# Token shares of the second feed-forward: turned in steps 6 to 12 of the block attention, from copies kept among the constants

## The chip, the cores and the metric

The kernel runs on one core of a Trainium2 chip. The metric is the device time of one execution in microseconds (us), the median over several runs. The engines are TensorE (PE in the profile; its weight loads are PEld), VectorE (DVE), ScalarE (ACT), GpSimd (POOL) and SyncE (SP), which only issues transfers here. Each runs its own list of instructions in order and waits on semaphores.

## The reference

Two transformer layers over x of 4 x 256 tokens by 256. Each layer adds an attention and a mixture of experts to x. The change lies in the second layer:

```
xn = layernorm(x)
# attention: 16 heads of 16, keys in blocks of 32 tokens, each query sees its 4 best blocks
mask   = selected blocks & causal
p      = softmax(where(mask, q @ k.T * d**-0.5, NEG));  o = p @ v
o      = o * rsqrt(mean(o*o)) * o_norm_w;  attn = o @ Wo.T
# feed-forward: 8 experts of rank 32, two for each token
rw, sel = top_k(softmax(x @ Wg.T), 2);  rw = rw / rw.sum(-1)
for k in range(2):
    x1, x3 = base1 + lora1[sel[:, k]], base3 + lora3[sel[:, k]]
    x2  = silu(x1) * x3
    out += (x2 @ W2.T + lora2(x2)) * rw[:, k]
```

The two numbers rw of a token are its shares. The kernel multiplies x2 by them while the tokens lie along the free axis, so it needs each share repeated over all 128 partitions.

## The kernel before, in words

All is written out by hand: each engine has a function with its instructions in order, and semaphores order the work between them. No planner moves anything.

At the end of the second layer's preparation VectorE chooses the two experts and forms `share` (line 1748). It then writes the block scores (lines 1753 to 1756, the last of them steps the semaphore `blk_step` to 3) and ranks the blocks: 7 comparisons of the first batch's heads (`compare`, line 691), 14 additions and subtractions (`count`, lines 700 and 702), and four comparisons of the other heads. GpSimd copies `share` into `share_rep`, each share repeated 128 times along the free axis: two copies of 1024 elements per partition (line 905). It goes on with its own rankings once VectorE has done all seven comparisons of the other heads, then with masks, with the splitting of the expert weights `b13` into a high and a low part (lines 924 and 927), and with further splits for the feed-forward.

The block attention runs over steps j = 0 to 34. A step has two heads, n = 2j and 2j + 1, and four heads (two steps) make a quad Q. On TensorE a step is: the scores of its heads (`scores1`, lines 2206 and 2212); in odd steps from 3 the products with the values of quad (j - 3) // 2 (`values1`, line 2233); the turning of the probabilities of the step before (`probs1_turn`, line 2222, six transposes); in even steps from 4 the turning of a quad's output (`quad_turn`, line 2241). ScalarE in a step takes the exponents of one head (`exponents`, line 1198, two instructions), copies the turned probabilities of the even head (line 1204), takes the exponents of the other head, and in some steps scales the next queries (`own_queries`, line 1167), forms the next block bias (`own_bias`, line 1178) and copies a quad's output (`quad_out`, line 1214). VectorE adds the bias to the scores and takes their minimum (`masked_minimum`, line 1774), copies the odd head's turned probabilities (line 1783) and divides the quad's heads (`heads_out`, lines 1789 and 1792).

Into the first steps the kernel puts the shares. TensorE turns `share_rep` by four transposes for a quarter of it (`shares(n)`, line 2341) into a PSUM bank, and ScalarE copies the bank to `shareT` (`share_out(n)`, line 1208), which the feed-forward reads. `share_rep` lies in the same place as the later slots of `probs1T`, the turned probabilities, so it has to be read before they are written. Quarter 0 uses bank 2 and quarters 1 to 3 bank 7, which are also the two banks of the values and the quad outputs. In step 5 TensorE waits until all four quarters have left their banks. Scores use banks 3, 4, 0 and 1, turned probabilities banks 5 and 6.

Behind step 31 TensorE goes straight on to the feed-forward's hidden layer (`hidden1`), which wants GpSimd's splits.

Of the kernel before, what the change touches and what calls it, by code (L numbers as in the profile page):

```python
# [15 lines left out]
ACT = mybir.ActivationFunctionType  # L16
AX = mybir.AxisListType

P = 128
B, S, D = 4, 256, 256  # L20
TOK = B * S
NT = TOK // P
# [48 lines left out]
HG = H1 // 2  # L71
QUADS = 2 * GROUPS
VW = D1 + 1
SCORE_BANK, SHARE_BANK = (3, 4, 0, 1), (2, 7, 7, 7)

F1, E1, R1 = 896, 8, 32
ER = E1 * R1
# [1 line left out]
CH = 512  # L79
# [56 lines left out]
B3_AT = -(-CF["q_cos"][0] // ALIGN) * ALIGN  # L136
# [160 lines left out]
def program(nc, t, y):  # L297

    ctx = ExitStack()
    with ctx:  # L300
# [31 lines left out]
        with ExitStack() as overlay:  # L332
            end = 0
            kept, phase = -(-(CF_N + BC_N + NT * D) // ALIGN) * ALIGN, start[1] + 8 * TOK
# [23 lines left out]
        sb = ctx.enter_context(nc.sbuf_tensor("sb", [P, SB_COLS], F32))  # L358
        rd = ctx.enter_context(nc.sbuf_tensor("rounded", [P, ROUNDED], F32))
        cb = ctx.enter_context(nc.sbuf_tensor("cb", [P, CB_N], BF16))  # L360
        bank = [ctx.enter_context(nc.psum_tensor(f"bank{i}", [P, 512], F32)) for i in range(8)]
# [7 lines left out]
        region2 = whole.take(REGIONS[2])  # L369
# [17 lines left out]
        def tableb(name):  # L387
# [3 lines left out]
        ident, identb = table("ident"), tableb("ident")  # L391
# [110 lines left out]
        phase = r2.at  # L502
# [5 lines left out]
        r2 = Strip(region2, phase + 2 * NT * D, NT * D)  # L508
        expert_of = [r2.take_b(NT, ER) for _ in range(2)]
        one_of = [bias_g[:, k].rearrange("p q n -> p (q n)")[:, 0:NT * E1].rearrange("p (t e) -> p t e", e=E1) for k in range(2)]  # L510
        share_rep = Strip(region2, phase + 3 * NT * D, 2 * NT * P).take(2 * NT, P)
        r2 = Strip(region2, phase, region2.shape[1] - phase)
        v_last = r2.take(H1, VW)
        v_one = [v_most[:, i] for i in range(NT - 1)] + [v_last]
# [21 lines left out]
        shareT = r4.take(2, TOK)  # L536
# [13 lines left out]
                           for w in (w13, w13_lo[:, :].rearrange("p (k n) -> p k n", k=KD)))  # L550
# [56 lines left out]
        kmean_set, kmean_done, blk_mm, blk_step = (sem(n) for n in ("kmean_set", "kmean_done", "blk_mm", "blk_step"))  # L607
# [4 lines left out]
        fill_mm, fill_out, step_mask, low_rank = (sem(n) for n in ("fill_mm", "fill_out", "step_mask", "low_rank"))  # L612
        bl_q, bl_bias, bl_s, bl_min, bl_exp, bl_inv, bl_t, bl_even, bl_odd, bl_v, bl_oT, bl_turn, bl_o = (
            sem(n) for n in ("bl_q", "bl_bias", "bl_s", "bl_min", "bl_exp", "bl_inv", "bl_t", "bl_even", "bl_odd", "bl_v",
                             "bl_oT", "bl_turn", "bl_o"))
# [17 lines left out]
        def fills():  # L633

            out = [("low", j, h, c) for j in range(2) for h in range(2) for c in range(TOK // CH)]
            return out + [("mask", k, h, c) for k in range(2) for h in range(2) for c in range(TOK // CH)]
# [164 lines left out]
        def _(pool):  # L801
# [8 lines left out]
            for u in range(2 * NF):  # L810
                n = P if u // 2 < NF - 1 else FH
# [69 lines left out]
            for i in range(NT):  # L881
# [3 lines left out]
                if i >= HALF:  # L885
                    n, k = (i - HALF) // KD, (i - HALF) % KD
# [14 lines left out]
            for q in range(QT):  # L901
                pool.tensor_copy(ranks_b[:, q], along(table("later", QT, NB)[:, q], (1, B), (2, H1))).then_inc(kmean_set, 1)
            pool.wait_ge(r1_step, 10 + 2 * NT)
            for k in range(2):
                pool.tensor_copy(share_rep[:, k * NT:(k + 1) * NT, :], along(share[:, :, k], (2, P))).then_inc(r1_share, NT)

# [12 lines left out]
                pool.tensor_tensor(am_step[j], am_step[j], step_maskT, ALU.mult).then_inc(low_rank, 1)  # L919

            pool.wait_ge(ab_in, 48)
            for j in range(2):
                for h in range(2):
                    pool.tensor_copy(r(b13_hi[j][h]), b13[:, h, j * F1:(j + 1) * F1]).then_inc(b13_split, 1)
                for h in range(2):
                    pool.wait_ge(b13_split, 4 * j + h + 1)
                    pool.tensor_tensor(r(b13_lo[j][h]), b13[:, h, j * F1:(j + 1) * F1], b13_hi[j][h], ALU.subtract)\
                        .then_inc(b13_split, 1)
# [31 lines left out]
        def _(act):  # L960
# [63 lines left out]
            for u in range(2, 2 * NF):  # L1024
# [3 lines left out]
                if 0 <= u - 3 < NT:  # L1028
                    i = u - 3
# [171 lines left out]
            def even_probsT(n):  # L1201
                act.wait_ge(bl_t, n + 1)
                at_least(act, bl_v, n // 4 - 1)
                act.activation(probs1T[:, n % 8, :], bank[5][:, 0:3 * P], ACT.Copy).then_inc(bl_even, 1)

            def share_out(n):
                act.wait_ge(fill_mm, len(fills()) + n + 1)
                act.activation(shareT[:, n // 2, n % 2 * CH:(n % 2 + 1) * CH], bank[SHARE_BANK[n]][:, :], ACT.Copy)\
                    .then_inc(fill_out, 1)

            def quad_out(Q):
# [18 lines left out]
            for j in range(2 * QUADS + 3):  # L1230
                if j < 2 * QUADS:
                    exponents(2 * j)
                if 0 < j <= 2 * QUADS:
                    even_probsT(2 * j - 2)
                if j == 2 * QUADS:
                    act.wait_ge(bl_s, GROUPS * HG)
                    act.wait_ge(w3_in, 32)
                    high_part("w13", 1)
                    high_part("w13", 2)
                    activated(0, 0)  # L1240
                if j < 2 * QUADS:
                    exponents(2 * j + 1)
                if 0 < j < 5:
                    share_out(j - 1)
                if j % 4 == 2 and j // 4 + 1 < GROUPS:
                    own_queries(j // 4 + 1)
                if j % 4 == 3 and j // 4 + 1 < GROUPS:
                    own_bias(j // 4 + 1)
                if j % 2 and j > 2:
                    quad_out((j - 3) // 2)  # L1250
# [621 lines left out]
        def _(pe):  # L1872
# [14 lines left out]
            for i in range(NT):  # L1887
# [5 lines left out]
                for k in range(KD):  # L1893
                    mm = pe.matmul(bank[4 + i % 2][:, 0:LATX], xnT[:, k, i * P:(i + 1) * P], w_lat[:, k, 0:LATX],  # L1894
                                   start=(k == 0), stop=(k == KD - 1))
# [31 lines left out]
            for u in range(2 * NF):  # L1927
                shared_up(u)
                if u == 2 * NF - 2:
# [5 lines left out]
                    for i in range(NT - 1):  # L1935
                        mm = pe.matmul(bank[6][:, (i + 1) * E0:NT * E0].rearrange("p (t e) -> p t e", e=E0),
                                       tableb("ones"), along(maskb[:, i, :], (1, NT - 1 - i)),
                                       start=False, stop=(i == NT - 2), skip_group_check=True)
# [132 lines left out]
            for i in range(NT):  # L2071
# [9 lines left out]
                for f in range(NF):  # L2081
                    mm = pe.matmul(bank[DOWN_BANK[i]][:, 0:D], hT[:, f, i * P:(i + 1) * P], sw_down[:, f, :],  # L2082
                                   start=(f == 0), stop=(f == NF - 1))
# [13 lines left out]
                if i == NT - 2:  # L2097
                    for j in range(NT * TOPK0):
                        if j % HOT == 0:
                            pe.wait_ge(rt_mask, j // HOT + 2)  # L2100
                        mm = pe.matmul(bank[7][:, 0:2 * E0].rearrange("p (h e) -> p h e", h=2), hot[:, j, :], ids[:, :, j, :],
                                       start=(j == 0), stop=(j == NT * TOPK0 - 1))
# [112 lines left out]
            def probs1_turn(n):  # L2215
                pe.wait_ge(bl_exp, 2 * n + 2)
                if n % 2:
                    at_least(pe, bl_odd, (n - 1) // 2)
                else:
                    at_least(pe, bl_even, n // 2)  # L2220
                for j in range(3):
                    mm = pe.transpose(bank[5 + n % 2][:, j * P:(j + 1) * P], probs1[:, n % 4, j * P:(j + 1) * P], ident)  # L2222
                mm.then_inc(bl_t, 1)

            def values1(Q):
                G, b, k, par, i = place_of(4 * Q)
                pe.wait_ge(bl_even, 2 * Q + 2)
                pe.wait_ge(bl_odd, 2 * Q + 2)
                at_least(pe, bl_o, Q - 1)
                for t_ in range(QT):  # L2230
                    for i in range(4):
                        dst = bank[2 + 5 * (Q % 2)][32 * i:32 * i + VW, t_ * P:S]
                        mm = pe.matmul(dst, v_one[QT * b + t_][:, HG * k + 2 * i + par, :],
                                       probs1T[:, (4 * Q + i) % 8, 2 * t_ * P:(2 + t_) * P],
                                       start=(t_ == 0), stop=(t_ == 1))
                mm.then_inc(bl_v, 1)
# [99 lines left out]

            def shares(n):
                pe.wait_ge(r1_share, 4 * n + 4)
                pe.wait_ge(fill_out, len(fills()) + (n if n > 1 else 0))
                for i in range(4):  # L2340
                    mm = pe.transpose(bank[SHARE_BANK[n]][:, i * P:(i + 1) * P], share_rep[:, 4 * n + i, :], ident)
                mm.then_inc(fill_mm, 1)

            pe.wait_ge(fill_out, len(fills()) - 3)
# [2 lines left out]
            for j in range(2 * QUADS + 3):  # L2347
                if j < 2 * QUADS:
                    scores1(j)
                if j == 1:  # L2350
                    shares(0)
                    shares(1)
                if j in (3, 4):
                    shares(j - 1)
                if j == 5:
                    pe.wait_ge(fill_out, len(fills()) + 4)
                if j % 2 and j > 2:
                    values1((j - 3) // 2)
                if 0 < j <= 2 * QUADS:
                    probs1_turn(2 * j - 2)  # L2360
                    probs1_turn(2 * j - 1)
                if j == 2 * QUADS:
                    hidden1(0)
                if j == 2 * QUADS + 1:
                    hidden1(1)
                if j % 2 == 0 and j > 3:
                    quad_turn((j - 4) // 2)
# [37 lines left out]
```

## Time and profile before

| what | value |
|---|---|
| median of 3 runs | 700.69 us (700.65 to 703.05) |
| the profiled execution | 701.29 us, of which the span from first to last instruction is 699.1 us |
| busy in the span | PE 96%, DVE 70%, ACT 61%, POOL 43% |
| granted TensorE clock | 1.00 |
| the block attention, from TensorE's first scores to its last probabilities | 408.0 to 493.6 us |

In a row of the timeline the first number is the start in us from the span's start, the second the length in us, then engine, line, operation, tiles and shapes, and the count of instructions that the row merges; in brackets stands how long the engine was idle before it and what released it. A record begins when the instruction is taken up, and the next one often begins before the end of the one before: what an instruction costs its engine is read from start to start. In a row of the windows stand the stretch and its length, then busy time and count of PE, PEld, DVE, ACT and POOL, then the granted clock, the DMA share and GB/s.

### The profile page before, as it was taken

Reading aid. Unit: us, or ns where it says so; the run is one execution under the profiler, and the core shown is the slowest. Engines: PE = TensorE matmul, PEld = TensorE weight load, DVE = VectorE, ACT = ScalarE, POOL = GpSimd, SP = SyncE. Lnnn points to the kernel's source line nnn. Section 1 sums busy time; section 2 is a strip of 40 time slices with the busy share of each in tenths; the row PEclk is TensorE's granted clock in tenths of the full one; section 3 lists DMA queues with packets and bytes.
Section 4 is the critical chain, followed back from the end, with each engine's and each line's share of the span. In section 5 each row is a group of like instructions: output and inputs, shape, how many; then the busy total and the mean of one; then the engine's idle time right before and its main releaser. Section 6 shows DMA issues by size and latency. Waiting matters only on the chain.

```text
span 699.1 us, 13847 instructions
## 1 busy us (share of the span) xinstructions
PE 671.0 (96%) x4756; PEld 581.7 (83%) x4756; DVE 489.0 (70%) x1418; ACT 424.3 (61%) x1099; POOL 297.8 (43%) x301
## 2 busy tenths in 40 slices
PE   6999999999999999999999989999989999999997
PEld 3777888888889898887787855666889999999997
DVE  6798877877877787777786886777465555644544
ACT  3766168788797878888663788888654213222221
POOL 0584154546464555542164318998334410400000
PEclk9999999999999999999999999999999999999999
DMA  8902044453535444351910000200300000000000
GB/s 329 346 1 98 1 130 121 165 166 112 168 116 165 129 152 126 101 159 59 365 79 1 1 1 2 107 1 3 121 1 1 1 1 16 2 16 1 1 16 16
DMA packets 26725, 59.43 MB, mean 85 GB/s; under 512 B 3146, under 2 KB 12748, under 8 KB 26272
## 3 DMA queue, kind: packets, MB, share of 16 engines
q1 hardware_dynamic: 23584, 50.35, 21.5%
q0 software_dynamic: 3072, 8.20, 3.6%
q8 instruction: 39, 0.64, 0.4%
q14 instruction: 30, 0.25, 0.1%
HBM read 48.24 MB, written 10.49 MB: 84 GB/s over the span
## 4 chain that ended last, share of the span: by engine, by line
PE 76%; DVE 14%; ACT 6%; issue 3%; POOL 1%; DMA 0%; DVEq 0%; ACTq 0%
PE bank L2253 11%; PE bank L2020 7%; PE bank L1954 6%; PE bank L2302 5%; PE bank L2011 5%; PE bank L2276 5%; PE bank L2040 4%; PE bank L1961 3%; PE bank L2031 3%; PE bank L2082 3%; PE bank L2316 2%; PE bank L2222 2%; PE bank L2206 2%; PE bank L1894 2%; PE bank L2161 2%
## 5 line engine op out<-in xcount | busy, mean ns | idle before, releaser
L1062 ACT ACTIVATE sb<-bank,sb 128x256 f32<-128x256 f32 x128 | 59.6, 471 | 40.6 <-DVE sb L1558 33.4
L1558 DVE TENSOR_REDUCE sb<-bank 128x2 f32<-128x512 f32 x64 | 43.7, 683 | 47.5 <-PE bank L2020 47.1
L1264 ACT ACTIVATE h_parts<-sb 128x256 fp32r<-128x256 f32 x56 | 23.4, 418 | 71.3 <-DVE sb L1809 43.4
L2020 PE MATMUL bank<-sb 128*128 128x256 f32 x256 | 66.2, 381 | 0.0
L1800 DVE TENSOR_TENSOR sb<-sb,bank 128x256 f32<-128x256 f32 x56 | 23.5, 419 | 58.1 <-ACT sb L1227 58.1
L2253 PE MATMUL bank<-rounded,b_hi 128*128 128x256 f32 x224 | 63.1, 282 | 0.0
L2253 PE MATMUL bank<-rounded,b_lo 128*128 128x256 f32 x224 | 62.9, 281 | 0.0
L2253 PE MATMUL bank<-am_lo,b_hi 128*128 128x256 f32 x224 | 62.9, 281 | 0.0
L1227 ACT ACTIVATE sb<-bank 128x256 f32<-128x256 f32 x56 | 21.5, 383 | 62.4 <-PE bank L2253 62.4
L834 POOL DMA_INDIRECT expert_out<-sb x32 | 33.0, 1032 | 61.0 <-DVE sb L1500 44.6
L1069 ACT ACTIVATE sb<-sb 128x256 f32<-128x256 f32 x128 | 57.7, 503 | 0.1
L1198 ACT ACTIVATE sb<-sb 128x128 f32<-128x128 f32 (+1 forms) x128 | 50.6, 445 | 10.1 <-DVE sb L1774 9.4
L1954 PEld LDWEIGHTS bank<-sb 128*128 128x128 f32 (+1 forms) x384 | 46.5, 186 | 5.8 <-DVE sb L1494 3.2
L828 POOL DMA_INDIRECT sb<-rows_x,sb x32 | 32.8, 1025 | 42.4 <-PE bank L1954 16.4
L1954 PE MATMUL bank<-sb 128*128 128x128 f32 (+1 forms) x384 | 48.8, 277 | 1.7 <-DVE sb L1494 1.0
L2020 PEld LDWEIGHTS bank<-sb 128*128 128x128 f32 x256 | 45.2, 190 | 4.8
L1774 DVE CUSTOM_DVE_ANT_1 sb<-bank,sb 128x128 f32<-128x128 f32 (+1 forms) x128 | 38.0, 353 | 12.8 <-ACT sb L1178 8.5
L1569 DVE TENSOR_TENSOR pt_parts<-bank,pt_parts 128x512 fp32r<-128x512 f32 x64 | 43.7, 683 | 4.5 <-ACT pt_parts L1082 3.6
L2040 PE MATMUL bank<-pt_parts,xt_parts 128*128 128x256 f32 x256 | 46.0, 302 | 0.0
L1811 DVE TENSOR_TENSOR h_parts<-sb,h_parts 128x256 fp32r<-128x256 f32 x56 | 25.9, 462 | 27.4 <-ACT h_parts L1264 27.4
L2011 PE MATMUL bank<-rounded 128*128 128x512 f32 x160 | 42.7, 399 | 0.3 <-ACT sb L1091 0.3
L2253 PEld LDWEIGHTS bank<-rounded,b_lo 128*128 128x128 f32 x224 | 42.2, 188 | 0.0
(321 smaller groups left out, 1969.9 us busy)
## 6 DMA issues: line engine op xcount, KB each, us to landing
sb<-in_w_gate_up SPq DMA_DIRECT2D x32, 368.0 KB
sb<-in_w_down SPq DMA_DIRECT2D x32, 256.0 KB
sb<-in_w_pair SPq DMA_DIRECT2D x8, 704.0 KB
expert_out<-sb SPq DMA_DIRECT2D x1, 4096.0 KB, 23.7
sb<-expert_out SPq DMA_DIRECT2D x8, 512.0 KB, 6.3
sb<-in_w SPq DMA_DIRECT2D x1, 1792.0 KB, 13.8
sb<-in_b SPq DMA_DIRECT2D x1, 1792.0 KB, 8.1
sb<-in_sw_up SPq DMA_DIRECT2D x1, 1536.0 KB, 9.4
```

The source lines that it names most:

```text
L1062: act.activation(probs[:, u % 4, q, :], bank[3 + u % 2][:, q * S:(q + 1) * S], ACT.Exp, scale=-1.0, bias=row_min[:, u % 4, q:q + 1], accum ...
L1069: ins = act.activation(probs[:, slot, q, :], probs[:, slot, q, :], ACT.Copy, scale=row_inv[:, slot, q:q + 1])
L1198: act.activation(probs1[:, n % 4, a:b], masked[:, n % 4, a:b], ACT.Exp, scale=-1.0, bias=row_min[:, n % 4, q:q + 1]).then_inc(bl_exp, 1)
L1558: dve.tensor_reduce(row_min[:, u % 4, :], bank[3 + u % 2][:, :].rearrange("p (q n) -> p q n", q=QT), AX.X, ALU.min).then_inc(at_min, 1)
L1569: dve.tensor_tensor(r(probs_lo[:, u % 2]), bank[5 + u % 2][:, :].rearrange("p (a b) -> p a b", a=QT), probs_hi[:, u % 2], ALU.subtract).th ...
L1774: dve.tensor_tensor_reduce(masked[:, n % 4, a:b].rearrange("p (n c) -> p n c", c=CHUNK), bank[SCORE_BANK[n % 4]][:, a:b].rearrange("p (n c ...
L1954: mm = pe.matmul(bank[1][0:n, to:to + P], w_gu[s][:, k, a:a + n], xeT[s][:, k, :], start=(k == 0), stop=(k == KD - 1))
L2011: mm = pe.matmul(where[:, :], r(w[i][:, cols]), r(q[:, half]), start=(n == 0), stop=(n == len(terms) - 1))
L2020: mm = pe.matmul(bank[3 + u % 2][:, q * S:(q + 1) * S], qb[i][:, h, b * S + q * P:b * S + (q + 1) * P], keys[:, h, b * S:(b + 1) * S], sta ...
L2040: mm = pe.matmul(bank[2 + 5 * h][:, 0:S], r(v_parts[:, QT * b + k, :]), r(part[:, u % 2, k, :]), start=(n == 0), stop=(n == len(terms) - 1))
L2253: mm = pe.matmul(dst, lhs, rhs, start=False, stop=(n == len(terms) - 1), skip_group_check=True)
L2276: pe.matmul(dst, r(w[:, 2 * k + j, :]), r(x[:, k, :]), start=(i + j == 0), stop=False, skip_group_check=True)
```

## The change

`share_rep` moves from the place under `probs1T` to the columns of the constants from `B3_AT` on: rotation tables, block masks and layer-norm rows that are done with by then. Later the same columns take the high parts of `b13` (second half) and one tile of another weight. GpSimd's two copies therefore wait until VectorE has read the block masks (`blk_step` 3), and GpSimd waits, ahead of splitting `b13`, until all four quarters have been turned. The quarters are turned in steps 6, 8, 10 and 12 instead of 1, 1, 3 and 4, alternately in banks 2 and 7, right behind the scores; each waits until the quad that had the bank is done (`bl_o`). ScalarE copies a quarter in the same step, between its copy of the turned probabilities and the second exponents. In steps 7, 9, 11 and 13 TensorE first turns the probabilities, then waits for the quarter's copy and forms the values; in the other odd steps the order stays.

```diff
-SCORE_BANK, SHARE_BANK = (3, 4, 0, 1), (2, 7, 7, 7)
+SCORE_BANK = (3, 4, 0, 1)
+SHARE_AT = {6: 0, 8: 1, 10: 2, 12: 3}
...
-        share_rep = Strip(region2, phase + 3 * NT * D, 2 * NT * P).take(2 * NT, P)
+        share_rep = Strip(sb, B3_AT, 2 * NT * P).take(2 * NT, P)
...
             pool.wait_ge(r1_step, 10 + 2 * NT)
+            pool.wait_ge(blk_step, 3)
             for k in range(2):
                 pool.tensor_copy(share_rep[:, k * NT:(k + 1) * NT, :], along(share[:, :, k], (2, P))).then_inc(r1_share, NT)
...
             pool.wait_ge(ab_in, 48)
+            pool.wait_ge(fill_mm, len(fills()) + 4)
...
             def share_out(n):
                 act.wait_ge(fill_mm, len(fills()) + n + 1)
-                act.activation(shareT[:, n // 2, n % 2 * CH:(n % 2 + 1) * CH], bank[SHARE_BANK[n]][:, :], ACT.Copy)\
+                act.activation(shareT[:, n // 2, n % 2 * CH:(n % 2 + 1) * CH], bank[2 + 5 * (n % 2)][:, :], ACT.Copy)\
                     .then_inc(fill_out, 1)
...
                     even_probsT(2 * j - 2)
+                if j in SHARE_AT:
+                    share_out(SHARE_AT[j])
...
                     exponents(2 * j + 1)
-                if 0 < j < 5:
-                    share_out(j - 1)
...
             def shares(n):
                 pe.wait_ge(r1_share, 4 * n + 4)
-                pe.wait_ge(fill_out, len(fills()) + (n if n > 1 else 0))
+                pe.wait_ge(bl_o, n + 1)
                 for i in range(4):
-                    mm = pe.transpose(bank[SHARE_BANK[n]][:, i * P:(i + 1) * P], share_rep[:, 4 * n + i, :], ident)
+                    mm = pe.transpose(bank[2 + 5 * (n % 2)][:, i * P:(i + 1) * P], share_rep[:, 4 * n + i, :], ident)
                 mm.then_inc(fill_mm, 1)
...
                 if j == 1:
-                    shares(0)
-                    shares(1)
-                if j in (3, 4):
-                    shares(j - 1)
-                if j == 5:
-                    pe.wait_ge(fill_out, len(fills()) + 4)
-                if j % 2 and j > 2:
+                    pe.wait_ge(fill_out, len(fills()))
+                if j in SHARE_AT:
+                    shares(SHARE_AT[j])
+                behind_shares = j - 1 in SHARE_AT
+                if j % 2 and j > 2 and not behind_shares:
                     values1((j - 3) // 2)
                 if 0 < j <= 2 * QUADS:
                     probs1_turn(2 * j - 2)
                     probs1_turn(2 * j - 1)
+                if behind_shares:
+                    pe.wait_ge(fill_out, len(fills()) + SHARE_AT[j - 1] + 1)
+                    values1((j - 3) // 2)
```

## Rows read from the trace of the kernel before

**Rows 1.** Windows: one period of four steps, 6 to 9.
```profile
426.12:436.40 10.28, 10.17 (x103) 6.44 (x102) 7.51 (x40) 8.97 (x26) 8.64 (x22) 1.00 0.00 0
```
**Rows 2.** Timeline of PE, steps 1 to 6 and the start of step 10.
```profile
410.25 1.04 PE L2341 MATMUL bank<-sb 128*128 128x128 f32 x8
411.95 1.24 PE L2222 MATMUL bank<-sb 128*128 128x128 f32 x6 [0.67 <-ACT sb L1198]
413.12 0.92 PE L2206 MATMUL bank<-sb 32*128 32x128 f32 x8
...
417.47 0.63 PE L2341 MATMUL bank<-sb 128*128 128x128 f32 x4 [1.27 <-ACT sb L1208]
...
421.19 0.63 PE L2341 MATMUL bank<-sb 128*128 128x128 f32 x4 [0.34 <-ACT sb L1208]
421.66 0.82 PE L2222 MATMUL bank<-sb 128*128 128x128 f32 x6
422.31 0.38 PE L2241 MATMUL bank<-sb 128*128 128x128 f32 x2
...
424.54 0.84 PE L2233 MATMUL bank<-sb 128*17 128x256 f32 x16 [0.67 <-ACT sb L1208]
425.32 0.87 PE L2222 MATMUL bank<-sb 128*128 128x128 f32 x6
426.12 0.92 PE L2206 MATMUL bank<-sb 32*128 32x128 f32 x8
...
436.30 0.92 PE L2206 MATMUL bank<-sb 32*128 32x128 f32 x8
```
**Rows 3.** Timeline of ACT, steps 0 to 2.
```profile
411.10 2.18 ACT L1198 ACTIVATE sb<-sb 128x128 f32<-128x128 f32 x6 [1.42 <-DVE sb L1774]
...
416.75 0.58 ACT L1208 ACTIVATE sb<-bank 128x512 f32<-128x512 f32 x1
417.22 0.90 ACT L1167 ACTIVATE sb<-sb 128x256 f32<-128x256 f32 x2
```
**Rows 4.** Timeline of ACT, steps 6 to 8.
```profile
427.98 0.80 ACT L1198 ACTIVATE sb<-sb 128x128 f32<-128x128 f32 x2 [0.63 <-DVE sb L1774]
428.68 0.47 ACT L1204 ACTIVATE sb<-bank 128x384 f32<-128x384 f32 x1
429.05 0.79 ACT L1198 ACTIVATE sb<-sb 128x128 f32<-128x128 f32 x2
429.75 0.90 ACT L1167 ACTIVATE sb<-sb 128x256 f32<-128x256 f32 x2
430.55 0.79 ACT L1198 ACTIVATE sb<-sb 128x128 f32<-128x128 f32 x2
...
432.30 0.39 ACT L1178 ACTIVATE sb<-sb 128x128 f32<-128x128 f32 x1
...
433.49 0.80 ACT L1198 ACTIVATE sb<-sb 128x128 f32<-128x128 f32 x2 [0.54 <-DVE sb L1774]
```
**Rows 5.** Timeline of DVE and POOL around the copies, before the first step.
```profile
399.72 1.05 POOL L905 COPY sb<-sb 128x1024 f32<-128x1024 f32 x1
...
400.01 1.82 DVE L1756 TENSOR_TENSOR sb<-sb 128x1024 f32<-128x1024 f32 x1
...
407.94 2.56 DVE L691 TENSOR_TENSOR sb<-sb 128x672 bf16<-128x672 f32 x4
```
**Rows 6.** Timeline, elsewhere: DVE with two SBUF inputs, first or behind POOL.
```profile
357.47 2.05 POOL L889 TENSOR_TENSOR w_qkvg_lo<-sb,w_qkvg_hi 128x776 fp32r<-128x776 f32 x1
...
357.86 1.94 DVE L1669 SCALAR_TENSOR_TENSOR sb<-sb 128x256 f32<-128x256 f32 x1
...
531.54 1.22 DVE L1857 TENSOR_TENSOR sb<-sb 128x1024 f32<-128x1024 f32 x1
```
**Rows 7.** Timeline of POOL: before its rankings, first split of b13, before the feed-forward.
```profile
416.14 0.60 POOL L700 TENSOR_TENSOR sb<-sb 128x224 f32<-128x224 f32 x1 [15.37 <-DVE sb L691]
...
457.64 1.81 POOL L924 CAST b_hi<-sb 128x896 fp32r<-128x896 f32 x2
...
494.23 2.52 POOL L956 TENSOR_TENSOR w_lo<-sb,w_hi_rest 128x512 fp32r<-128x512 f32 x2 [6.67 <-ACT w_hi_rest L1219]
```

## The prediction, made before the changed kernel was run

> **What bounds the kernel now.** I read the page first, for the shares of the engines, and then the chain of work that ended last. TensorE has most of that chain over the whole span, so the question is only what the change does to TensorE's time between its first scores and the hidden layer behind step 31. The windows of that stage come next. In a period of four steps TensorE is busy 10.17 of 10.28 us and ScalarE 8.97 [rows 1]: from step 6 on TensorE is the bound, and ScalarE is not far behind. The period is 10.18 us, from the scores of step 6 at 426.12 to those of step 10 at 436.30, while steps 2 to 5 took 13.00 us, from 413.12 to 426.12 [rows 2]. The timeline says why: in these steps TensorE is idle three times for the copy of a quarter, 1.27, 0.34 and 0.67 us [rows 2]. The reader is to see two regimes: early steps with holes, later ones without.
>
> The timeline of VectorE shows a third thing. It has no gap ahead of the first minimum: its last four comparisons run from 407.94 for 2.56 us [rows 5], the first minimum follows at once, at about 410.4, and ScalarE was idle 1.42 us for it before the first exponents at 411.10 [rows 3], for which TensorE in turn was idle 0.67 us [rows 2]. So whatever delays VectorE ahead of step 0 delays the whole stage.
>
> **What is removed from the early steps.** Quarters 0 and 1 in step 1 (eight transposes, 410.25 to 411.29) lie in a hole: TensorE had to wait until 411.95 for exponents anyway [rows 2]. Removing them gives nothing. Quarter 2 in step 3 costs its wait of 1.27 us and about 0.5 of transposes, quarter 3 in step 4 costs 0.34 and 0.47 (421.19 to 421.66), and step 5 waits 0.67 [rows 2]: some 3.3 us on TensorE, the most that can be won. What comes up in its place are the waits that every later period has: steps 2 and 3 hold the same scaled queries and bias on ScalarE as steps 6 and 7. I therefore take the period of 10.18 as what steps 2 to 5 will need, and the gain as 13.00 - 10.18 = 2.8 us. It was 0 if another wait filled these holes. Against that: ScalarE's copies of the quarters (0.47 us each, from 416.75 to 417.22 [rows 3]) leave its list there as well, and the probabilities that the values of step 3 want were copied before the hole of 1.27 us had ended.
>
> **What is added to steps 6 to 13.** On TensorE each quarter is four transposes, 0.47 us by the distance to the next row [rows 2], and TensorE has 0.11 us of idle time in a period. The four cost at least 4 x 0.47 = 1.9 us. The changed order makes it a little more, because the second transposes of a step now wait for exponents that ScalarE takes behind a quarter's copy, with no values in front of them to cover that. Worked out on ScalarE, which sets the pace there:
>
> - Steps 6 and 7. From the exponents at 427.98 to those at 433.49 are 5.51 us of exponents (0.70), copy (0.37), exponents (0.70), queries (0.80) and so on; the last piece, from the bias at 432.30 by way of VectorE's minimum, is 1.19 us [rows 4]. Up to the bias ScalarE has no gap. The quarter's copy adds 0.47 and nothing absorbs it: +0.5.
> - Steps 8 and 9. From the exponents at 433.49 to the scores of step 10 at 436.30 were 2.81 us. After the change the path is: exponents 0.70, copy 0.37, quarter 0.47, exponents 0.70 [rows 3, 4], then on TensorE half of the six transposes, 0.33 of 0.65 (421.66 to 422.31), and the values, 0.78 (424.54 to 425.32) [rows 2], with some 0.05 from engine to engine: 3.4 us. That is +0.6.
>
> Together 1.1 us for four steps, 2.2 us for steps 6 to 13. The other bound is that every quarter is paid with a wait like that of step 5 on top of its transposes, 4 x (0.47 + 0.67) = 4.6 us. I take 2.2, since it follows the new order of instructions. The waits on `bl_o` cost nothing: quad 0 is divided in step 4 and quarter 0 asks in step 6, and so on two steps apart. From step 14 on the order is the old one.
>
> One page of the Trainium skill would give another price. "TensorE: Matmul & The Clock Gate", in its part on PE-mode transpose, gives about 275 ns for one transpose in a kernel. The records here have the same length, but four of them start within 0.47 us of each other and the next work. Taken one after another, 16 x 0.275 = 4.4 us would be an estimate from that page, and the sum would be 2.2 us higher than mine; the distance between rows decides.
>
> **The copies on GpSimd.** They are two instructions of 1.05 us. Before, the second ran from 399.72 to 400.77, and VectorE's L1756, taken up at 400.01, needed 1.82 us, where the same shape in L1857 needed 1.22 [rows 5, 6]. It ended 1.06 us behind the copy: it stood still until the copy was over. The same is seen at L1669: taken up at 357.86 beside GpSimd's L889, which ended at 359.52, it ended at 359.80 [rows 6]. In both cases VectorE has two inputs in SBUF and GpSimd reads SBUF too. After the change the copies start behind L1756, so this one gets back 0.6 us. They then run beside the seven comparisons and the additions of the ranking, which all have two inputs in SBUF. The comparison that is under way holds GpSimd for a moment, then a copy holds the next comparison, and at its end the turn changes again; L889 took its turn in this way between two instructions of VectorE. So both copies are paid: 2 x 1.05, less about 0.1 for the overlap, = 2.0 us. With the 0.6 regained VectorE reaches the first minimum 1.4 us later, at 411.8, and the stage starts 1.4 us later. The bounds are -0.6 (VectorE keeps its turn until it is through) and +1.5. I take 1.4.
>
> The Trainium skill, "SBUF — State Buffer", in "Who interferes with whom", says the same of a VectorE instruction with two SBUF inputs beside a GpSimd instruction that reads SBUF: one is blocked for the whole of the other. No row has a comparison (L691) beside a GpSimd instruction, and the page puts it with the others. By it the sum would be 2.1 for 2.0 us; a reading in which bf16 outputs escape would take away 2.0.
>
> **What costs nothing.** GpSimd's own list: the copies move some 2.5 us later into a wait of 15.37 us [rows 7]. That wait ends with VectorE's last comparison in step 2, so the rankings and all behind them start 1.4 us later too; ahead of the feed-forward GpSimd then waited another 6.67 us [rows 7]. Its new wait for the fourth quarter stands before the splitting of `b13` at 457.64 [rows 7], when step 12 (half a period behind step 10, about 441) is long past; were it ever late, the splits would hold the hidden layer. SyncE has no new wait; its weights for the feed-forward are released by the last scores and move with the stage.
>
> **The sum.** -2.8 + 2.2 + 1.4 = +0.8 us in the span: 699.1 becomes 699.9, and the profiled execution 702.1. That execution was 0.6 us above the median of the runs; on the median 700.69 I forecast 701.4 us, +0.1%.
>
> **Rivals.**
>
> 1. The comparisons aren't held by the copies. For it: GpSimd has no priority that the rows show, and each comparison is short. Against: L1756 and L1669. Then -2.8 + 2.2 - 0.6 = -1.2: 699.4 us.
> 2. The quarters cost more than the order of instructions says, 4.6 us instead of 2.2, because ScalarE (8.97 of 10.28 us busy) becomes the bound in steps 6 to 13. Against: 0.47 us in two steps still fits into its idle time by count. Then +3.2: 703.9 us.
> 3. The early steps don't get shorter: VectorE's and ScalarE's start-up sets steps 2 to 5, and the holes stay under other names. Then 0 + 2.2 + 1.4 = +3.6: 704.3 us, slower by 0.5%. It decides from the point where less than 0.1 us of the 2.8 is won. Against: all three holes name the copy of a quarter.
> 4. The moved work is free and the copies too: -2.8 - 0.6, 697.3 us. TensorE's 0.11 us of idle time speaks against it.
>
> **How the numbers follow.** The forecast with small shifts of its terms 0.62, rival 1 0.16, rival 2 0.12, rival 3 0.06, rival 4 0.04. The range takes in the forecast, rival 1, the lower half of rival 2, and a run-to-run change of a few tenths: 699.1 to 703.1. By 0.5% (3.5 us), about what a measurement of this kernel can tell from no change, only rival 3 and a worse rival 2 are slower, and only a rival 4 with more is faster: faster 0.02, same 0.92, slower 0.06.
>
> **What the profile after should show.** No idle time of TensorE for L1208 in steps 2 to 5, and about 10.2 us from the scores of step 2 to those of step 6. About 11.3 us each for steps 6 to 9 and 10 to 13, with TensorE idle 0.8 to 0.9 us ahead of the turned probabilities in steps 9 and 13, released by L1198, and 10.2 us again from step 14. L1756 at 1.2 us; two comparisons or additions behind it with 1 us more than before; the first minimum at about 411.8. Wrong would be: comparisons of unchanged length, periods of over 12 us with quarters, or a first period still near 13 us.

## The result: 0.65% slower, and where the time went

The changed kernel takes 705.24 us (median of 9 runs, 704.36 to 709.56), the kernel before 700.69 us in 9 runs beside it. The ratio is 1.0065, 95% interval 1.0053 to 1.0077: 4.6 us slower, where 701.4 us (699.1 to 703.1) was forecast. The profiled execution took 704.72 us with a span of 702.8 us, 3.7 us more than before. Eight of the nine executions took 704.4 to 705.5 us with a mean granted clock of 0.992, the ninth 709.56 us with 0.983.

All of it lies in the block attention. The windows of the kernel after, in the columns explained above: from the first scores to the first turned probabilities, then the rest of steps 1 to 3 and the start of 4, steps 4 and 5, and the periods 6 to 9, 10 to 13 and 14 to 17.

```profile
407.48:412.60 5.12, 2.43 (x20) 1.28 (x21) 4.96 (x19) 2.61 (x7) 0.00 (x0) 0.90 0.01 2
412.60:422.20 9.60, 9.58 (x55) 5.95 (x55) 5.02 (x27) 6.05 (x17) 3.72 (x8) 0.52 0.01 3
422.20:427.02 4.82, 4.82 (x52) 3.18 (x51) 3.74 (x20) 4.13 (x13) 4.04 (x11) 1.00 0.00 0
427.02:438.52 11.50, 10.75 (x110) 7.25 (x109) 8.19 (x41) 10.45 (x31) 9.70 (x24) 1.00 0.01 2
438.52:450.02 11.50, 10.74 (x112) 7.25 (x108) 7.64 (x40) 9.83 (x29) 11.34 (x5) 1.00 0.44 162
450.02:460.20 10.18, 10.07 (x104) 6.33 (x100) 6.95 (x39) 8.36 (x25) 10.18 (x4) 1.00 0.01 2
```

The third number from the end of a row is the granted clock. In the second row it is 0.52 while TensorE is busy all the time: for some 9 us it ran at 1.2 instead of 2.4 GHz. The 0.90 of the first row is about 1.0 us more of it, at the end of the hole. That is what no step of the prediction had. The timeline of TensorE shows what it had done before, beside [rows 2]:

```profile
407.48 0.92 PE L2209 MATMUL bank<-sb 32*128 32x128 f32 x8
...
412.62 1.51 PE L2225 MATMUL bank<-sb 128*128 128x128 f32 x6 [2.71 <-ACT sb L1201]
414.06 1.65 PE L2209 MATMUL bank<-sb 32*128 32x128 f32 x8
...
419.58 1.48 PE L2236 MATMUL bank<-sb 128*17 128x256 f32 x16
...
427.02 0.92 PE L2209 MATMUL bank<-sb 32*128 32x128 f32 x8
...
431.27 0.55 PE L2225 MATMUL bank<-sb 128*128 128x128 f32 x3 [0.19 <-ACT sb L1201]
...
437.27 0.55 PE L2225 MATMUL bank<-sb 128*128 128x128 f32 x3 [0.56 <-ACT sb L1201]
...
438.52 0.92 PE L2209 MATMUL bank<-sb 32*128 32x128 f32 x8
```

The hole ahead of the first turned probabilities is 2.71 us long instead of 0.67: the eight transposes of quarters 0 and 1 are gone from it, and VectorE is later. The scores of step 2 then take 1.65 us instead of 0.92, and none of the holes for a quarter's copy is left in steps 2 to 5. Still these steps take 12.96 us (414.06 to 427.02) where they took 13.00. The timeline of VectorE and GpSimd around the copies, beside [rows 5]:

```profile
399.51 1.22 DVE L1759 TENSOR_TENSOR sb<-sb 128x1024 f32<-128x1024 f32 x1
400.77 3.22 DVE L692 TENSOR_TENSOR sb<-sb 128x224 bf16<-128x224 f32 x7
...
411.00 0.28 DVE L1777 CUSTOM_DVE_ANT_1 sb<-bank,sb 128x128 f32<-128x128 f32 x1
```
```profile
400.89 2.29 POOL L907 COPY sb<-sb 128x1024 f32<-128x1024 f32 x2 [11.46 <-DVE sb L1759]
```

The last addition to the block scores is back at 1.22 us (1.82 before), and the seven comparisons beside the copies take 3.22 us.

From row to row the 4.0 us that the stage grew from its first scores to those of step 14 divide so (the stage of before began 0.5 us later in its span, which is why the span grew less):

| stretch, from scores to scores | before | after |
|---|---|---|
| step 0 to 2 | 5.14 | 6.58 |
| step 2 to 6 | 13.00 | 12.96 |
| step 6 to 10 | 10.18 | 11.50 |
| step 10 to 14 | 10.18 | 11.50 |
| step 14 to 18 | 10.18 | 10.18 |

### The profile page after: what moved, and what is told of

It is laid out like the page before. It is cut to its first block, busy times and chain, and to the rows that moved or that the text cites. A ratio compares the mean times of both kernels' runs of the same rounds, so it can differ in the third digit from the quotient of the medians.

```text
span 702.8 us, 13853 instructions
## 1 busy us (share of the span) xinstructions
PE 673.7 (96%) x4756; PEld 584.1 (83%) x4756; DVE 490.2 (70%) x1418; ACT 424.0 (60%) x1099; POOL 297.9 (42%) x301
## 4 chain that ended last, share of the span: by engine, by line
PE 73%; DVE 16%; ACT 6%; issue 4%; POOL 1%; DMA 0%; DVEq 0%; ACTq 0%
PE bank L2256 11%; PE bank L2023 7%; PE bank L1957 6%; PE bank L2305 5%; PE bank L2014 5%; PE bank L2279 5%; PE bank L2043 3%; PE bank L1964 3%; PE bank L2034 3%; PE bank L2085 3%; PE bank L2225 2%; PE bank L2319 2%; PE bank L2209 2%; PE bank L2164 2%; PE bank L1897 2%
## 5 line engine op out<-in xcount | busy, mean ns | idle before, releaser
L1201 ACT ACTIVATE sb<-sb 128x128 f32<-128x128 f32 (+1 forms) x128 | 50.4, 446 | 14.6 <-DVE sb L1777 14.4
```

Of the source, the lines that this page charges most:

```text
L1201: act.activation(probs1[:, n % 4, a:b], masked[:, n % 4, a:b], ACT.Exp, scale=-1.0, bias=row_min[:, n % 4, q:q + 1]).then_inc(bl_exp, 1)
```

## The experiments

Theory A: the hole on TensorE makes the clock fall, and the low clock takes the gain of steps 2 to 5. Rival B: VectorE and ScalarE set steps 2 to 5 whatever the clock, or the clock falls for something else. Ratios are to the kernel before, with 95% intervals; the table below has the stretches of each profile.

**Eight transposes put back.** The kernel after with

```diff
                 if j == 1:
                     pe.wait_ge(fill_out, len(fills()))
+                    for i in range(8):
+                        pe.transpose(bank[2 + 5 * (i // 4)][:, i % 4 * P:(i % 4 + 1) * P], ident, ident)
```

> The kernel after, with eight transposes of the identity in step 1, where the two quarters stood before; their results are never read. Theory A (the clock): the hole ahead of the first turned probabilities was 2.71 us long and the granted clock fell behind it, to a mean of 0.52 for 9.6 us. Eight transposes make the hole about 1.7 us, the clock stays at 1.00, steps 2 to 5 take 10.2 us instead of 12.96 and the first turning another 0.3 less: 705.2 - 3.1 = 702.1 us. Rival B (start-up): steps 2 to 5 take 13 us because VectorE and ScalarE set them, whatever the clock: 705.2 us.

Measured: 703.71 us (12 runs), 1.0023 [1.0011, 1.0034]. The hole was 1.76 us and the clock fell nevertheless, but later:

```profile
412.00:416.00 4.00, 3.13 (x21) 2.38 (x22) 3.36 (x21) 3.37 (x10) 0.00 (x0) 0.86 0.00 0
416.00:420.00 4.00, 4.00 (x30) 1.70 (x28) 2.45 (x13) 3.21 (x9) 2.77 (x5) 0.50 0.00 0
```

So A's forecast failed in the profile: with a hole of 1.76 us the clock still fell. But the profiled execution is one of eight, at 703.3 to 704.3 us and a mean clock of 0.994 or 0.995; the other four took 701.9 to 702.5 us, about the 702.1 of theory A, at 0.999. With this hole the clock falls in most executions and not in all. B isn't excluded by the profile, since steps 2 to 5 took 12.49 us.

**Copies later on GpSimd.** The kernel after with

```diff
             pool.wait_ge(blk_step, 3)
+            pool.wait_ge(bl_min, 1)
```

> The kernel after, with GpSimd's two copies held back until the first minimum of step 0 is done, when no VectorE instruction with two SBUF inputs is under way. Theory A: the seven comparisons take 1.5 us again instead of 3.2, L1759 keeps its 1.22, the first minimum comes 2.3 us behind the first scores instead of 3.5, the hole on TensorE is about 1.4 us and the clock stays at 1.00. The sum against before is -2.8 (steps 2 to 5) - 0.5 (first minimum) + 2.6 (steps 6 to 13, two periods of 11.50 instead of 10.18) = -0.7: 700.0 us. Rival B: steps 2 to 5 stay at 13 us, 702.8 us. If a hole of 1.4 us without any transposes in it is enough for the clock to fall: about 703.

Measured: 703.28 us (12 runs), 1.0029 [1.0014, 1.0044]. The part about VectorE came true; its timeline:

```profile
399.97 1.23 DVE L1760 TENSOR_TENSOR sb<-sb 128x1024 f32<-128x1024 f32 x1
401.23 1.56 DVE L692 TENSOR_TENSOR sb<-sb 128x224 bf16<-128x224 f32 x7
...
410.37 0.28 DVE L1778 CUSTOM_DVE_ANT_1 sb<-bank,sb 128x128 f32<-128x128 f32 x1
410.58 0.42 DVE L1778 CUSTOM_DVE_ANT_1 sb<-bank,sb 128x256 f32<-128x256 f32 x1
```
```profile
410.27 2.03 POOL L908 COPY sb<-sb 128x1024 f32<-128x1024 f32 x2 [20.37 <-DVE sb L1778]
```

The comparisons take 1.56 instead of 3.22 us with nothing but the time of the copies changed, and the minima (L1778), which run beside the copies now, have the 0.28 of the kernel after. The hole shrank to 1.08 us, but the clock fell again, and for longer (the mean was 0.50 from 412.3 to 425). So the 700.0 us were missed and the last sentence of the expectation, about 703 us, came true. The profiled execution took 706.43 us, one of four at 705.6 to 706.4 us (mean clock 0.988 or 0.989); the other eight took 702.3 to 703.5 us (0.992 or 0.993), so the 15.51 us in the table below is the worse kind.

**The place alone.** The kernel before with `share_rep` in the constants and GpSimd's two waits:

```diff
-        share_rep = Strip(region2, phase + 3 * NT * D, 2 * NT * P).take(2 * NT, P)
+        share_rep = Strip(sb, B3_AT, 2 * NT * P).take(2 * NT, P)
...
+            pool.wait_ge(blk_step, 3)
...
+            pool.wait_ge(fill_mm, len(fills()) + 4)
```

> The kernel before with one part of the change: the repeated shares among the constants, with the two waits on GpSimd that go with it. The quarters stay in steps 1, 1, 3 and 4. Theory A: the copies hold VectorE as in the kernel after, the first minimum is 1.1 us later, the hole on TensorE grows from 0.67 to 1.7 us, the clock stays at 1.00: 700.7 + 1.1 = 701.8 us. If a hole of 1.7 us is enough for the clock: some 3 us more, 704.8. If the copies' delay is absorbed: 700.7.

Measured: 703.50 us (12 runs), 1.0025 [1.0015, 1.0034]. The hole became 1.76 us:

```profile
412.85 1.24 PE L2224 MATMUL bank<-sb 128*128 128x128 f32 x6 [1.76 <-ACT sb L1200]
414.02 0.92 PE L2208 MATMUL bank<-sb 32*128 32x128 f32 x8
...
416.40 1.65 PE L2208 MATMUL bank<-sb 32*128 32x128 f32 x8
```

Steps 0 and 1 took 6.24 us instead of 5.14: the copies' price is 1.1 us. And the clock fell here too, with every quarter where it had been. This part alone makes the kernel slower, by 0.25%; the 704.8 us that the expectation gave for a fallen clock were more than was measured.

**The quarter's copy behind the second exponents.** The kernel with late copies and

```diff
                     even_probsT(2 * j - 2)
-                if j in SHARE_AT:
-                    share_out(SHARE_AT[j])
...
                     exponents(2 * j + 1)
+                if j in SHARE_AT:
+                    share_out(SHARE_AT[j])
```

> As the kernel with late copies, and ScalarE copies a quarter behind the second exponents of its step instead of ahead of them. TensorE's second transposes in steps 7, 9, 11 and 13 then don't wait for the quarter; the values behind them do. By the order of instructions that saves 0.2 us in steps 7 and 11 and 0.3 to 0.5 us in steps 9 and 13, about 1 us: 699.0 us where the late copies alone give 700.0. Rival: the quarter's 0.48 us on ScalarE is on the path wherever it stands: no difference between the two.

Measured: 703.08 us (12 runs, 697.69 to 704.33), 1.0001 [0.9981, 1.0020]. The periods with quarters took 11.03 us instead of 11.50, 0.95 us in all, as expected: the place of the copy in ScalarE's list has its price. The total tells little, since ten executions took 701.2 to 704.3 us (mean clock 0.990 to 0.993) and two 697.7 and 697.9 (1.000). In the profiled one, of the long kind, the clock was down behind a hole of 1.05 us:

```profile
409.90:411.10 1.20, 0.15 (x3) 0.04 (x1) 1.20 (x9) 0.95 (x3) 1.18 (x2) 1.00 0.00 0
411.10:421.90 10.80, 10.72 (x60) 6.76 (x62) 5.66 (x28) 7.27 (x21) 5.66 (x11) 0.53 0.01 2
```

**The hole filled.** Three experiments asked whether the clock was all of it. First the kernel after with 20 transposes in the place of 8:

```diff
                 if j == 1:
                     pe.wait_ge(fill_out, len(fills()))
+                    for i in range(20):
+                        pe.transpose(bank[2 + 5 * (i // 4 % 2)][:, i % 4 * P:(i % 4 + 1) * P], ident, ident)
```

> The kernel after, with 20 transposes of the identity in step 1 in place of 8, some 2.5 us of work that nobody reads; it fills the hole of 2.71 us almost wholly. With 8 of them a hole of 1.76 us was left, and the clock fell all the same from 415 on. Theory A (TensorE's idle time between its first scores and the first turned probabilities makes the clock fall, and the clock takes the gain of steps 2 to 5): clock 1.00 throughout the stage, steps 2 to 5 take 10.2 us, median about 701.5 us. Rival B (the clock falls for the work ahead of the first scores, or for the kind of work, transposes among it): it falls again, 704 us or more.

Measured: 701.82 us (11 runs, 701.59 to 702.50), 1.0011 [1.0002, 1.0020]. The timeline and the windows:

```profile
409.79 2.35 PE L2356 MATMUL bank<-sb 128*128 128x128 f32 x20
412.59 1.24 PE L2225 MATMUL bank<-sb 128*128 128x128 f32 x6 [0.45 <-ACT sb L1201]
413.76 0.92 PE L2209 MATMUL bank<-sb 32*128 32x128 f32 x8
```
```profile
407.50:412.60 5.10, 4.62 (x41) 3.50 (x41) 4.93 (x20) 2.58 (x7) 0.00 (x0) 1.00 0.02 5
412.60:423.90 11.30, 10.64 (x104) 6.79 (x104) 8.72 (x47) 9.98 (x29) 6.02 (x15) 1.00 0.00 1
```

The clock stays at 1.00 in the stage, and steps 2 to 5 take 10.18 us. Work that nobody reads makes the kernel 0.54% faster by the ratios, 3.8 us. Rival B falls in each of its forms: nothing on VectorE or ScalarE was changed, nor the work ahead of the first scores, and the added work is transposes.

Then the reverse on the kernel before: two of the eight transposes of quarters 0 and 1 are left in step 1.

```diff
-                for i in range(4):
+                for i in range(4 if n > 1 else 1):
```

> The kernel before, in which quarters 0 and 1 are turned by one transpose each instead of four (six of the eight transposes of step 1 are left out, so half of the tokens' first shares are not formed). Nothing else moves: VectorE and ScalarE have the same times, and the hole ahead of the first turned probabilities grows from 0.67 to about 1.4 us. Theory A: the clock falls, steps 2 to 5 take 14 to 15.5 us instead of 13.0, and the median is 2 to 3 us above before. Rival B (these transposes lay in a hole and are worth nothing, as the prediction had it): the same time as before.

(Of the first shares one in four is formed, not half.) Measured: 703.29 us (6 runs, 702.15 to 705.13), 1.0035 [1.0022, 1.0048]. The windows of the hole, of what follows, of the low clock and of the rest up to step 6:

```profile
409.70:411.00 1.30, 0.01 (x1) 0.01 (x1) 1.30 (x11) 0.87 (x3) 0.00 (x0) 1.00 0.00 0
411.00:417.00 6.00, 4.59 (x36) 2.99 (x36) 4.97 (x27) 5.85 (x16) 1.66 (x3) 1.00 0.01 3
417.00:420.70 3.70, 3.70 (x30) 2.44 (x30) 0.56 (x1) 2.17 (x7) 3.15 (x8) 0.54 0.01 2
420.70:426.10 5.40, 4.81 (x52) 3.13 (x48) 3.29 (x19) 4.26 (x12) 4.54 (x12) 1.00 0.00 0
```

Taking work away made the kernel 2.5 us slower, as theory A said. The profile is of the fastest of the six executions: its steps 2 to 5 took 0.96 us more than before, and the clock fell once more at the start of the feed-forward (last section), so that the time behind the scores of step 14 grew by another 0.9 us. Steps 0 and 1 still took 5.13 us, so the six transposes had indeed lain in a hole, and were not free to remove all the same. The clock did not fall behind the first hole but behind the second, the 1.27 us in step 3 that the kernel before has too [rows 2] and gets over in its profile. Not in each of its executions, it seems: of the 75 of the kernel before that ran beside the experiments, 19 had a mean clock of 0.992 to 0.995 and took 701.9 to 703.3 us. No profile shows where the clock fell in them.

Last, four more transposes in step 1 of the kernel before:

```diff
                     shares(1)
+                    for i in range(4):
+                        pe.transpose(bank[6][:, i * P:(i + 1) * P], ident, ident)
```

> The kernel before with four more transposes of the identity in step 1, 0.5 us for its hole of 0.67 us. The clock didn't fall there in the profile. Theory A: nothing changes in the median, 0 to -0.5 us; a filler that isn't needed costs nothing. Rival: four transposes delay the chain of step 1, +0.5 us.

Measured: 701.19 us (12 runs), 1.0003 [0.9994, 1.0012], the stretches as before. A filler inside a wait costs nothing, and brings nothing where the clock stands. Nor did these four keep the clock up everywhere: five of the twelve executions had a mean clock of 0.993 or 0.995 and took 701.9 to 703.3 us.

**Versions that beat both.** The kernel with late copies and the later quarter's copy, plus the eight transposes of the first experiment:

> The kernel with late copies and the quarter's copy behind the second exponents, plus eight transposes of the identity in step 1, about 1 us, for the hole of 1.05 us. Without them ten of twelve executions took 701.2 to 704.3 us and two took 697.7 and 697.9. Theory A: the clock stays in all of them, steps 2 to 5 take 10.2 us instead of 13.7, and the median is about 698 us, some 0.4% under before: a version that beats both. Rival B: about 703 us as before.

Measured: 699.27 us (11 runs, 697.41 to 699.87), 0.9974 [0.9965, 0.9983]. That is 1.3 us over the forecast: only two executions, 697.4 and 697.7 us, had a mean clock of 1.000; nine had 0.997 or 0.998 and took 698.7 to 699.9. In the profile, one of the nine, the clock stays at 1.00 in this stage and falls at the start of the feed-forward (last section). The hole is filled:

```profile
409.27 1.04 PE L2357 MATMUL bank<-sb 128*128 128x128 f32 x8
410.37 1.24 PE L2226 MATMUL bank<-sb 128*128 128x128 f32 x6
411.54 0.92 PE L2210 MATMUL bank<-sb 32*128 32x128 f32 x8
```

Beside the next one and the unchanged kernel after, on one chip:

> The version with late copies, the quarter's copy behind the second exponents and eight filler transposes, beside the last one on one chip: 0.997 times before, 699.3 us.

Measured: 699.51 us (5 runs), 0.9974 [0.9962, 0.9986]. And with real work as the filler (beside the lines shown, only the addresses of the two places and the waits on `bl_o` differ):

```diff
-SHARE_AT = {6: 0, 8: 1, 10: 2, 12: 3}
+SHARE_AT = {6: 2, 8: 3}
...
-        share_rep = Strip(sb, B3_AT, 2 * NT * P).take(2 * NT, P)
+        share_rep = [Strip(region2, phase + 3 * NT * D, NT * P).take(NT, P), Strip(sb, B3_AT, NT * P).take(NT, P)]
...
             for k in range(2):
+                if k == 1:
+                    pool.wait_ge(blk_step, 3)
+                    pool.wait_ge(bl_min, 1)
...
+                if j in (1, 2):
+                    share_out(j - 1)
...
                 if j == 1:
                     pe.wait_ge(fill_out, len(fills()))
+                    shares(0)
+                    shares(1)
+                if j in (3, 5):
+                    pe.wait_ge(fill_out, len(fills()) + (j - 1) // 2)
```

> Quarters 0 and 1 are copied to the old place and turned in step 1 as in the kernel before, where their eight transposes do what the filler did; quarters 2 and 3 are copied to the constants once the first minimum is done and are turned in steps 6 and 8, and ScalarE copies every quarter behind the second exponents. No filler. Theory A: the clock stays, step 2 begins 4.6 us behind the first scores, steps 2 to 5 take 10.2 to 10.7 us, steps 6 to 9 take 11.0 and steps 10 to 13 again 10.2. Against before -0.6 - 2.5 + 0.85 = -2.2 us, 0.8 us under the version with the filler: about 698.5 us. If the two copies of ScalarE in steps 1 and 2 are on its path, up to 1 us more. Rival B: the clock falls, 701 us or more.

Measured: 698.59 us (5 runs, 698.26 to 699.29), 0.9961 [0.9949, 0.9973]: 0.4% under the kernel before. Steps 2 to 5, 6 to 9 and 10 to 13 took 10.70, 11.02 and 10.18 us.

> The kernel after, unchanged, beside the next two on one chip: 1.0065 times before, that is 705 us, with the clock at 1.2 GHz for some 9 us in steps 1 to 5 in its profile.

Measured: 709.35 us (6 runs, 705.53 to 710.26), 1.0107 [1.0088, 1.0126]. The 705 us were missed. The same kernel lost more, because the clock stayed down twice as long: five of the six executions took 709.2 to 710.3 us with a mean clock of 0.983, and only one was like most of the first nine (705.53 us, 0.992). The profile is of the long kind:

```profile
409.30:412.00 2.70, 0.01 (x1) 0.00 (x0) 2.70 (x14) 0.91 (x3) 0.00 (x0) 0.66 0.00 0
412.00:430.70 18.70, 18.67 (x104) 11.56 (x104) 8.96 (x47) 10.71 (x30) 11.39 (x26) 0.50 0.01 1
```

All profiles together, in us (the repeat of "the same, 8 fillers" is left out, it agrees within 0.01); "hole" is TensorE's idle time ahead of the first turned probabilities:

| kernel | hole | step 0 to 2 | 2 to 6 | 6 to 10 | 10 to 14 | clock fell in these steps |
|---|---|---|---|---|---|---|
| before | 0.67 | 5.14 | 13.00 | 10.18 | 10.18 | no |
| before, 4 fillers | 0.22 | 5.13 | 12.99 | 10.17 | 10.18 | no |
| before, two of eight | 1.31 | 5.13 | 13.96 | 10.17 | 10.17 | yes |
| place alone | 1.76 | 6.24 | 14.44 | 10.18 | 10.18 | yes |
| after | 2.71 | 6.58 | 12.96 | 11.50 | 11.50 | yes |
| after, again | 2.73 | 6.60 | 17.23 | 11.51 | 11.50 | yes |
| after, 8 fillers | 1.76 | 6.23 | 12.49 | 11.51 | 11.50 | yes |
| after, 20 fillers | 0.45 | 6.23 | 10.18 | 11.50 | 11.51 | no |
| late copies | 1.08 | 4.71 | 15.51 | 11.50 | 11.51 | yes |
| late copies, order | 1.05 | 4.91 | 13.69 | 11.03 | 11.02 | yes |
| the same, 8 fillers | none | 4.54 | 10.18 | 11.03 | 11.02 | no |
| two and two | none | 4.55 | 10.70 | 11.02 | 10.18 | no |

## Why the prediction was wrong

**The step that failed:** "Quarters 0 and 1 in step 1 ... lie in a hole ... Removing them gives nothing." As time on the path that is right: with six of the eight gone, steps 0 and 1 kept their 5.13 us. But the transposes also kept the granted clock up. Without them, or with the hole stretched by the later minimum, the clock fell to 1.2 GHz in every profile with a hole of 1.05 us or more, and stayed at 1.00 in this stage in every one with 0.67 us or less. The profiles of the kernel after and of the one with 20 fillers differ by 0.35 us in steps 0 and 1 and by 2.78 us in steps 2 to 5, 3.1 us; the ratios 1.0065 and 1.0011 differ by 0.54%, 3.8 us. No rival had this. Rival 3 named the right outcome, steps 2 to 5 that don't get shorter and 704.3 us, by a wrong cause and so by luck: that the low clock cost just what the missing waits had won holds for one profile of the kernel after and not for the other.

**Steps 2 to 5, -2.8 us.** Right once the clock stands: 13.00 became 10.18 us with the hole filled, -2.82. With the clock down it was -0.04 in one profile and +4.23 in another of the same kernel.

**Quarters in steps 6 to 13, +2.2 us.** The mechanism was right, the size was 2.64 us (2 x 1.32). ScalarE's chain through steps 6 and 7 grew as worked out, from 5.51 to 6.00 us. The piece from there to the scores of step 10 was 3.65 us instead of the 3.4 of the prediction: the last three transposes took 0.47 us (437.27 to the values at 437.74), not 0.33, and began 0.15 us, not 0.05, behind their exponents. The hole that was named for step 9, 0.8 to 0.9 us, was there with 0.56 us by the bracket and L1201 as the releaser; another of 0.19 us stood in step 7. The prediction had not asked whether another place for the copy on ScalarE would be cheaper; it was, by 0.47 us in each period.

**The copies, +1.4 us.** The mechanism was right and shown by itself: 3.22 us for the comparisons beside the copies, 1.56 without, with L1759 back at 1.22. They held VectorE 1.66 us, not 2.0, and the stage came out at +1.10 us (5.14 to 6.24 with the place alone) instead of +1.4; the first minimum came 3.5 us behind the first scores, where 3.8 had been forecast (411.8 less 407.98). The Trainium skill, "SBUF — State Buffer", "Who interferes with whom", had these comparisons among the instructions that a GpSimd read can hold, and the runs agree.

**The sum without the clock, +0.8 us.** The kernel after with 20 fillers shows it best. From the first scores to those of step 14 its profile has 39.4 us where the kernel before has 38.5: +0.9 us, made up of -2.8, +2.65 and +1.1, so two terms were off by 0.45 and 0.3 us in opposite directions, which is luck. Its ratio, 1.0011 or +0.8 us (0.1 to 1.4), fits, but is no clean check: the clock fell once in its profile at the start of the feed-forward, and behind the scores of step 14 it took 1.1 us more than the kernel before. In the recorded sum itself there is a slip: 700.69 + 0.8 is 701.5 and not 701.4, and rival 1's 699.4 should be 699.5. The waits on `bl_o` and GpSimd's later waits cost nothing, as said: GpSimd waited 8.51 us ahead of the feed-forward where it had waited 6.67 [rows 7].

**The chances.** 0.06 for slower was too little, since the forecast took every cover for the whole price of the covered work. A hole that grows on TensorE was in the forecast's own numbers (0.67 us, plus eight transposes of 1.04, plus 1.4 of delay, some 3 us), and it was never added up.

## What to carry to other kernels

Work on TensorE that fills a wait isn't free to move: before it is taken away, add up the hole that it leaves with every delay the change brings there, and look whether the trace has a hole of that length behind which the granted clock held. The trace of before had none: its longest hole is the one of about 2 us in the next section, and the sum here was 3 us. One profile isn't enough for it either; the mean clock of each execution says in how many it fell. When a change gives nothing although the waits that it aimed at are gone, compare the length of the same instruction before and after (0.92 and 1.65 us here) ahead of any theory about dependences. And a GpSimd instruction that reads SBUF belongs beside VectorE work that reads PSUM, not beside work with two SBUF inputs: with the late copies the minima beside them, which read a bank and SBUF, kept their 0.28 us.

## What the runs showed of the hardware

The length of a hole alone doesn't decide. Nor does the clock fall at a fixed distance from it: in the kernel after, again, it is down for part of the hole itself (0.66 from 409.30 to 412.00, with TensorE idle; that is some 1.8 us at 1.2 GHz), and with 8 fillers in the kernel after it fell some 2 us behind the hole, with TensorE at work (0.86 from 412 to 416). Further on, at the start of the feed-forward, TensorE stands still for about 2.1 us in every version. Behind it the clock held in four of the thirteen profiles (before, before with 4 fillers, after, after with 8 fillers) and fell in the other nine. The first two rows are of the kernel before, the others of the version with late copies and eight fillers:

```profile
520.00:522.00 2.00, 0.09 (x1) 0.00 (x0) 1.53 (x3) 0.69 (x2) 0.00 (x0) 1.00 0.00 0
522.00:524.00 2.00, 1.81 (x15) 1.84 (x16) 1.44 (x5) 1.01 (x3) 0.20 (x1) 1.00 0.00 0
```
```profile
517.30:519.50 2.20, 0.10 (x2) 0.07 (x1) 1.72 (x4) 0.69 (x2) 0.00 (x0) 1.00 0.00 0
519.50:523.50 4.00, 4.00 (x21) 4.00 (x22) 2.26 (x4) 1.03 (x3) 2.44 (x2) 0.57 0.00 0
```

Once down, the clock stayed down for 3.4 us here (0.57 over 4.00 us) and for 18.7 us in another profile while TensorE was busy throughout, and two executions of the same kernel differed in it (the two profiles of the kernel after, some 9 and 18.7 us of busy time). The times of 697.7 and 703 us for the kernel with late copies and the later quarter's copy go with it: their mean clocks were 1.000 and 0.990. The short ones have no profile. What decides between them stays open; no run here separates it, nor does any say whether the small matmuls of the masks and scores ahead of the hole have a part in it.

Transposes counted as work for the clock: 20 of them, alone in 2.4 us, kept it at 1.00. The Trainium skill, "TensorE: Matmul & The Clock Gate", in its part on PE-mode transpose, says that the full clock doesn't engage for them, since they don't count as busy in the same way. The measurement differs from that so far as they held a clock that was already full; no run here shows whether transposes alone would raise it.
